# Layer 0 attention: the two heads' score and maximum products interleaved, and the first averages moved

## What is computed

```python
def _gn(v, G=32, eps=1e-5):
    B_, H_, W_, C_ = v.shape
    g = v.reshape(B_, H_, W_, G, C_ // G)
    m = jnp.mean(g, axis=(1, 2, 4), keepdims=True)
    s = jnp.var(g, axis=(1, 2, 4), keepdims=True)
    return ((g - m) / jnp.sqrt(s + eps)).reshape(v.shape)

# layer 0, after q, k, v = heads(x @ W + b)
attn = jnp.einsum('bqd,bkd->bqk', q, k) / np.sqrt(HD)
attn = (attn.reshape(b * NH, h, w, h, w) + rel_bias_h[:, :, :, :, None] + rel_bias_w[:, :, :, None, :])
attn = jax.nn.softmax(attn.reshape(b * NH, hw, hw), axis=-1)
out = jnp.einsum('bqk,bkd->bqd', attn, v)

x = x + _L0_conv_ref(_gn(x), ...)
x = x + _L1_conv_ref(_gn(x), ...)
```

## Time and profile before

| | us |
|---|---|
| median of 3 runs | 3215.44 (3212.84 to 3217.96) |
| the profiled execution, its own time | 3214.5 |
| its span | 3212.7 |

### The profile page before, as it was taken

The page is one execution under the profiler, slowest core; times in us unless marked ns, Lnnn a source line. Parts: engine busy times, 40 slices in busy tenths (PEclk is TensorE's granted clock), DMA queues, the critical chain, the costliest instruction groups (busy, mean ns, idle before and its releaser), DMA issues.

```text
span 3212.7 us, 48955 instructions
## 1 busy us (share of the span) xinstructions
PE 3144.4 (98%) x20428; PEld 2349.5 (73%) x20428; DVE 1703.3 (53%) x1889; ACT 1225.6 (38%) x1397; POOL 1084.7 (34%) x618
## 2 busy tenths in 40 slices
PE   8999999999999999999999999999999999999999
PEld 6875658887787656888778766688777866668876
DVE  4447745446435774543734577444463457744434
ACT  2345542124234654213423465321342355532132
POOL 0037770025003786002400477600330057750042
PEclk9999999999999999999999999999999999999999
DMA  3211013114421101311432100221153111031113
GB/s 124 93 35 26 20 49 115 40 54 130 139 95 27 25 20 50 114 40 61 159 126 72 34 21 18 84 90 40 59 174 108 66 37 24 14 111 59 40 34 115
DMA packets 170520, 220.39 MB, mean 69 GB/s; under 512 B 113856, under 2 KB 126400, under 8 KB 170304
## 3 DMA queue, kind: packets, MB, share of 16 engines
q1 hardware_dynamic: 168768, 215.68, 21.4%
q10 hardware_dynamic: 1536, 1.57, 0.2%
HBM read 141.70 MB, written 50.33 MB: 60 GB/s over the span
## 4 chain that ended last, share of the span: by engine, by line
PE 89%; issue 4%; ACT 3%; POOL 2%; DVE 1%; DMA 0%; SPq 0%; ACTq 0%; POOLq 0%
PE score L1157 15%; PE score L1158 14%; PE score L1159 14%; PE lot L1314 13%; PE score L1279 10%; PE lot L1229 5%; PE lot L1232 3%; PE score L1286 3%; PE score L1292 2%; PE lot L1331 2%; POOL acc L568 2%; PE lot L1262 2%; ACT prob L748 1%; PE lot L1200 1%; PE lot L1157 1%
## 5 line engine op out<-in xcount | busy, mean ns | idle before, releaser
L568 POOL TENSOR_TENSOR acc<-acc,prob 128x1024 f32<-128x1024 f32 x288 | 712.9, 2475 | 208.1 <-ACT prob L748 180.9
L748 ACT ACTIVATE prob<-score 128x1024 f32<-128x1024 f32 (+3 forms) x576 | 517.6, 910 | 416.6 <-PE score L1292 292.6
L889 DVE TENSOR_REDUCE max_part<-lot 128x1 f32<-128x512 f32 x640 | 411.3, 685 | 156.3 <-PE lot L1232 156.3
L1157 PE MATMUL score<-a_hi,w_hi 128*128 128x512 f32 x1152 | 458.9, 398 | 12.9 <-DVE q_lo L1002 5.1
L1314 PE MATMUL lot<-prob,v 128*64 128x512 f32 (+4 forms) x2496 | 462.2, 513 | 5.3 <-ACT o_raw L647 3.7
L1158 PE MATMUL score<-a_lo,w_hi 128*128 128x512 f32 x1152 | 450.7, 391 | 0.0
L1159 PE MATMUL score<-a_hi,w_lo 128*128 128x512 f32 x1152 | 450.0, 391 | 0.0
L568 POOL TENSOR_TENSOR acc<-prob 128x1024 f32<-128x1024 f32 x48 | 120.1, 2502 | 833.6 <-ACT prob L748 833.6
L1157 PE MATMUL score<-w_hi,a_hi 128*128 128x256 f32 x1152 | 336.1, 292 | 0.0
L1314 PEld LDWEIGHTS lot<-prob,v 128*64 128x64 f32 x2496 | 165.6, 137 | 232.0 <-issue 193.0
L1158 PE MATMUL score<-w_lo,a_hi 128*128 128x256 f32 x1152 | 325.5, 283 | 0.0
(11 more groups left out here) (112 smaller groups left out, 5370.2 us busy)
## 6 DMA issues: line engine op xcount, KB each, us to landing
raw<-weights SPq DMA_DIRECT2D x96, 768.0 KB, 4.4
g_mem<-g SPq DMA_DIRECT2D x24, 1024.0 KB, 4.7
xin<-x_t SPq DMA_DIRECT2D x24, 512.0 KB, 6.4
xr<-x_t SPq DMA_DIRECT2D x24, 512.0 KB, 5.2
x_mem<-xr SPq DMA_DIRECT2D x24, 512.0 KB, 6.6
xr<-x_mem SPq DMA_DIRECT2D x24, 512.0 KB, 5.4
y_t<-xr SPq DMA_DIRECT2D x24, 512.0 KB, 6.9
recip<-recip SPq DMA_DIRECT2D x368, 32.0 KB, 1.9
```

Of the source, the lines that this page charges most:

```text
L568: nc.gpsimd.tensor_tensor(acc[:, :, a:b], with_, now, ALU.add).then_inc(added, 1)
L748: nc.scalar.activation(prob[:, ug % P_SLOTS, :, 0:b - a], score[:, u % 2, :, 0:b - a], ACT.Exp, scale=SCALE).then_inc(prob_ok, 1)
L889: nc.vector.reduce_max(max_part[:, t, part, h:h + 1], lot[:, (2 * n + h) % 3, :], AX.X)\
L1157: nc.tensor.matmul(out, w[0], a[0], start=first, stop=False)
```

## The change

It has three parts. (1) At a unit with a maximum ahead, the maximum and the scores are issued as seven mixed pairs: first the two products of head 0's maximum beside head 1's first two score products, then the scores of head 0 beside those of head 1 and, last, head 0's last two score products beside head 1's maximum. Each head of a maximum has its own wait for a bank (two halves back, `no - 2`) and its own signal (`half_mm`), for which DVE waits head by head. (2) At the start TensorE makes six products of ones into `score`, whose result nothing reads. (3) DVE takes the first group's differences right behind its aggregates and its variance behind the fourth tile's statistics, and TensorE's averages of the second three tiles move behind the second and third input tile of the first product. The reduced numbers of the maxima in the projections of layer 0 and in layer 1 (`max_no`) only rename their count.

```diff
+def max_no(f, p, k):
+    return f // 2 * (2 + PAIRS) * QT + f % 2 * 2 * QT + p * QT + k + 1
...
-                dve.wait_ge(max_mm, unit_no(f, p, k))
                 for h in range(2):
+                    dve.wait_ge(half_mm, 2 * n + h + 1)
                     nc.vector.reduce_max(max_part[:, t, part, h:h + 1], lot[:, (2 * n + h) % 3, :], AX.X)\
...
                 statistics(0, i)
                 if i == 2:
                     aggregate(0, 0)
+                    group_means(0, 0)
                 if i == 3:
-                    group_means(0, 0)
+                    group_variances(0, 0)
+                if i == 4:
+                    norm(0, 0)
+                    norm(0, 1)
+                    input_lo(0, 0)
             aggregate(0, 1)
-            group_variances(0, 0)
-            norm(0, 0)
-            norm(0, 1)
-            input_lo(0, 0)
-            group_means(0, 1)
             norm(0, 2)
             input_lo(0, 1)
             input_lo(0, 2)
+            group_means(0, 1)
             group_variances(0, 1)
...
+            def head_pass(f, n, h, e):
+                p, k = n // (2 * QT) + 1, n % (2 * QT)
+                no = 2 * (n + f // 2 * LAST * 2 * QT) + h
+                if e == 0:
+                    if h == 0:
+                        maximum_ready(f, p, k)
+                    if no > 2:
+                        pe.wait_ge(half_max_ok, no - 2)
+                last = maximum_pass(no % 3, f, p, k, h, e)
+                if e:
+                    last.then_inc(half_mm, 1)
+                    halves_issued[0] = no + 1
...
+                banks_free(int(u in (2, 10)))
+                pe.wait_ge(max_ok, maxima_issued[0])
+                for k in range(passes + 2):
+                    if k < 2:
+                        head_pass(f, n, 0, k)
+                    else:
+                        last = score_pass(k - 2, 0)
+                    if k == passes + 1:
+                        last.then_inc(score_ok, 1)
+                    if k < passes:
+                        bias_ready(k)
+                        score_pass(k, 1)
+                    else:
+                        head_pass(f, n, 1, k - passes)
...
+            pe.wait_ge(const_ok, 1)
+            one_column = ones[:, 0:1]
+            for n in range(WARM_UP):
+                nc.tensor.matmul(score[:, 0, 0, :], one_column.to_broadcast([128, 128]),
+                                 one_column.to_broadcast([128, HALF]), start=True, stop=True)
             mean_averages(0, 0)
             shift_averages(0, 0)
-            mean_averages(0, 1)
...
-                        if f % 2 and j == 0 and i == 1:
+                        if len(norm_parts(f)) > 1 and j == 0 and i == 1:
                             mean_averages(f, 1)
-                        if len(norm_parts(f)) > 1 and j == 0 and i == (2 if f else 0):
+                        if len(norm_parts(f)) > 1 and j == 0 and i == 2:
                             shift_averages(f, 1)
...
-                        for n in before:
-                            head_maximum(f, n, int(u in (2, 10)))
-                        scores(f, p, u)
+                        scores(f, p, u, *before)
                         for n in behind:
-                            head_maximum(f, n, 0)
+                            head_maximum(f, n)
```

More of the change, by code:

```diff
@@ L36 @@
 GROUPED = 4
+WARM_UP = 6
 ORDER = (list(range(QT)), [0, 7, 1, 6, 2, 5, 3, 4])
@@ L1217, in maxima_read, with maximum_ready, maximum_pass @@
                     pe.wait_ge(half_max_ok, halves_issued[0])
[L1219 to L1222 removed]
+            def maximum_ready(f, p, k):
                 if k == 0:
                     pe.wait_ge(b_first, first_no(f, p))
[L1225 removed]
+                    if f % 2:
                         pe.wait_ge(qk_hi_ok, f * TILES + CT + p + 1)
[L1227 to L1234 removed]
+            def maximum_pass(bank, f, p, k, h, e):
+                t, _, a, b = max_at(f % 2, k)
+                queries, rows = slice(t * 128, (t + 1) * 128), rows_of(h)
+                bias = b_lo[0] if f % 2 else b_hi[SET_OF[0][p]]
+                w, x = (bias[rows, queries], onehot[rows, a:b]) if e else (
+                    q_hi[rows, p, queries], k_hi[rows, p, a:b])
+                return nc.tensor.matmul(lot[:, bank, 0:b - a], w, x, start=(e == 0), stop=(e == 1))
             def maximum(f, p, k):
@@ L1272, in scores, with score_pass, bias_ready @@
                 ug = units_before(f, p) + u
+                passes = 4 if layer else 5
+                def score_pass(k, h):
+                    w = (k_hi, k_hi, k_lo, None, None)[k]
+                    x = (q_hi, q_lo, q_hi, b_hi[s], b_lo[s])[k]
+                    if k < 3:
+                        w, x = w[rows_of(h), p, keys], x[rows_of(h), p, a:b]
+                    else:
+                        w, x = onehot[rows_of(h), keys], x[rows_of(h), a:b]
+                    return nc.tensor.matmul(score[:, slot, h, 0:b - a], w, x,
+                                            start=(k == 0), stop=(k == passes - 1))
+                def bias_ready(k):
+                    if u == 0 and k == 3:
+                        pe.wait_ge(shifted, pair_no(f, p))
+                        if layer == 0:
+                            pe.wait_ge(b_hi_ok, f // 2 * PAIRS + p + 1)
+                    if u == 0 and k == 4:
+                        pe.wait_ge(b_lo_ok, f // 2 * PAIRS + p + 1)
                 if p == 0 and u < 2:
```

63 lines of the change are left out of this document (21 added, 42 removed).

## The result

| | us |
|---|---|
| before, median of 10 runs | 3213.93 (3209.02 to 3217.96) |
| the change, median of 10 runs | 3205.69 (3203.17 to 3208.82) |
| ratio | 0.9972, 95% interval 0.9964 to 0.9980 |
| the change, profiled execution | 3206.56, span 3204.8 |

The change is faster by 8.2 us, 0.28%. The forecast was 3217 us with a range from 3207, and no change: both were wrong. The first rival's second half names this time (3205) and both causes, but its number is partly luck: start and attention gained some 13 us, more than its 9, and falls of the clock, which it did not have, gave 5 back. One execution of `maximum_moved` (6,176 us) and two of the kernel before (4,639 and 7,379 us) took far longer than all others, and the ratios leave them out.

What follows compares the result with a forecast made beforehand. TensorE, busy 98% of the span, was taken as the bound. Start +2.6 us and attention 0 on the profiled 3214.5 us made 3217 us, no change that can be told, with a range of 3207 to 3224.

Steps and rivals of the forecast that it cites:

- The first rival's second half: Attention waits fall, maxima behind cost nothing, and the clock rises during the first twelve products: 3205 us; whole rival 0.15, half faster.
- The start: Time up to the dense products: first product 3.6 us sooner, given back by averages, late `a_lo` and slow products; +2.6 us.
- if the clock again takes 5.3 us, 12 run at 0.43: Start, behind the last averages: of 54 products left, 12 run at half clock and 42 at 0.227 us, to 48.9 us.
- the late second `a_lo`: Start, after the first six products: DVE delivers the second `a_lo` at 23.3 us, leaving TensorE 1.0 us idle.
- The chain to the first product: Start: line 843 runs ahead of POOL, the power starts at 15.55 us, and the first product at about 19.8, not 23.40.
- The lower bound (-4.6): Start's gain if the clock never falls after the ones: -4.6 us.
- The attention: Layer 0's attention: removed waits and the cost of maxima behind cancel; 0.0 us per image, between -1.8 and +1.3.
- The wait for v and unit 2 together: Attention's first pair: unit 0's scores wait for v, +0.3 us; unit 2's wait for a maximum's read shrinks, -0.5 us.
- Unit 15: Attention: TensorE idles while line 923 holds up DVE; waits one half further back save 0.7 us per image.
- Pairs 1 to 4: Attention, unit 4 of each of these pairs: a later bank removes 0.22 us each, -0.9 us for four.
- So +0.13 in 14 of the 15 cases, +1.8: Attention, maxima behind at u = 1, 5, 9: second head waits for its bank and weight load; +1.8 us per image.
- the fourth rival: Attention: mixed pairs are slower; at 0.005 us a pair it is +9 us, 3226; chance 0.08, three quarters of it slower.

Runs made afterwards that it cites:

- maximum_moved: The change, with the first pair's maximum of unit 14 made behind unit 12 so that DVE's shift is not waited for; 3198.15 us, ratio 0.9943.
- ones_only: The kernel before with only the six products of ones added ahead of the first averages; 3217.68 us, ratio 1.0008.
- mixed_only: The change with its mixed order, but the wait ahead of head 0 of a maximum as long as before; 3235.45 us in one run.
- the ones in the gap: The change with six more float32 products of ones in TensorE's 5.65 us idle time behind the first shift averages; 3207.36 us, ratio 0.9975.
- both averages' places: Two variants of the change: start's second averages behind the first input tile, 3208.93 us; layer 1's end averages behind four output products, 3205.36 us.
- the filled end: The change with one product of ones over 256 columns in the 0.41 us idle time at each end of layer 1; 3205.64 us, ratio 0.9970.
- The last two kernels: The change with unit 14's maximum made behind unit 12, 3198.15 us; the same plus a product of ones at the ends of layer 1, 3197.98 us.
- before_again: The kernel before, unaltered, run and profiled once more; 3213.65 us.
- attention_only: The kernel before with only the change's attention of layer 0, its start as before; 3208.83 us, ratio 0.9984.
- no_ones: The change without the six products of ones at the start; 3211.28 us, ratio 0.9993.

## Why the prediction was wrong

**The start: +2.6 predicted, -4.95 measured.** The failing step is "if the clock again takes 5.3 us, 12 run at 0.43". I had counted from the dense work behind the last averages, because the one rise that I could see stood there; the clock in fact rose over the first twelve products, at 22.6 us, and everything behind ran at full clock. By the step's own terms: the second averages and the shift averages cost 1.48 us each in place of 2.9 and 2.9 (2.8), six products between and six ahead of them 1.5 instead of 2.5 (2.1), the 12 slow products are gone (2.4), the late second `a_lo` costs 0.4 instead of 1.0 (0.6), and the first product is 0.3 early. These make 8.2 us. Against them stands 0.5 us that the forecast had not: at 33.26 TensorE waits for the `a_lo` of the fourth input tile. That leaves 7.7, where forecast and result are 7.55 apart. The chain to the first product was right. The clock was down at the first product, as forecast, but not for the reason given: it fell at 12.4 us, within the shift averages, ahead of the gap. What the forecast said of the ones, that they pay for the first averages alone, was wrong too: `ones_only` has the clock up 8 us earlier than the kernel before and is 3.6 us ahead with nothing else changed. Why ones that end at 8.7 us bring a rise at 26.4, with the clock down between, the runs do not show. The lower bound (-4.6) was near by accident, since it assumed a clock that never fell; in later profiles of the same start the gain is 3.5 to 4.7.

**The attention: 0.0 predicted, -2.0 in each image measured.** The wait for v and unit 2 together: -0.2 predicted, -0.23 measured. Unit 15: -0.7, and -1.04 measured. Pairs 1 to 4: -0.9, and -0.8. These were right. The failing step is "So +0.13 in 14 of the 15 cases, +1.8". The read ends where it was forecast, 1.52 us behind the unit's start (256.20, forecast 1.51). But the maximum behind follows 0.07 us after it, not 0.16 and a weight load, and 0.22 us after the product ahead of it (256.04, 256.26), though the second head's weight load is late: it starts at 256.25, and load and product overlap, as in the earlier trace rows. A unit with its maximum takes 1.58 us (254.68 to 256.26) instead of 1.61, so that mixed pairs, at 0.226 to 0.228 us, are slightly shorter, not longer: the fourth rival was the wrong way round. Over four units with their product with v nothing of this is left, 10.74 us before and with the change (from 285.66 us of the kernel before on); the waits make the whole 2.0. `mixed_only` shows that the effect which I feared exists and costs 0.09 us a time, one half further on.

**What I had not in the sum at all**: the falls of the clock. I had quoted, where the clock fell in the kernel before, and used it only for the start. In the two profiles, four falls for one give back 5 of the 13 us that the change gains. (The sum also left out the 0.9 us by which the median lay above the profiled execution, and which it names; 3218 would have been no nearer.)

**What stays open.** The two profiles of the kernel before have one fall and none, six of the change and its variants with both parts' order kept (the change twice, the ones in the gap, both averages' places, the filled end) have three or four.

But two profiles say too little of the kernel before. Its 74 other executions on record have a mean granted clock of 0.997 to 1.000, 0.9988 on average, and the lower it is, the longer they take: 3211.7 us on average at 1.000 (20 executions), 3217.0 at 0.998 (22). My estimate from this: a mean of 0.9988 is 7.6 us at 1.2 GHz, some two falls in an execution, since one lasts 3.4 us in the windows; the change's ten executions have 0.9964, 23 us, of which the start has 10.2, so some three and a half. By this the falls cost the change some 2.5 us more than the kernel before, not 5, and part of the way from 13 to 8 us stays unexplained.

All 49 falls behind the start in the profiles stand at one of four kinds of place: the end of layer 1 (0.40 us of idle time, then averages of 4 columns), the shift of a first pair (1.36 us idle), the last pair of layer 1's attention (1.26 us idle for ACT's `prob`, then 0.2), and averages of 2 columns with 0.3 to 2.0 us idle. Most such places pass without a fall. The last two kernels, with the second kind taken away, have one fall each in their profiles. That a filled place has none, and that the falls move from it, rests on one profile each. Why the kernel before, with the same light places, falls less often stays open. With the change the falls at the ends of images are 795.3 us apart, so that each image meets the clock as the last did; but the images of the kernel before follow after 795.1 and 794.8 us too, so that this decides it is a guess.

## What to carry to other kernels

A stage that runs at half clock is not only priced by its length: ask what work stands together while the clock is low, and keep narrow averages and idle time out of the first wide products. A wait that hides another must be priced again when the order changes: the mixed order takes 5.8 us more in an image with the old wait than with the new one. And when a gain of 13 us shows as 8, look through the granted clock along the whole span, not only where the diff is, and at the mean clock of all runs, not of two profiles; a stall that stands in the list of waits with 5.4 us in 4 waits was worth 7.5 us, nearly as much as the whole change.

## What the runs showed of the hardware

- The granted clock of a window is 1.00 in the profile of a kernel until the first change of the clock is recorded: in `before_again`, the window from 29.40 to 32.80 (below) has 1.00 while its products are 0.43 us apart, and in the change, whose clock rose with the ones and fell, 19.20 to 22.60 has 0.50 with the same products. The distance of two products tells the level, the column does not.

```profile
29.40:32.80 3.40, 3.40 (x9) 2.63 (x9) 2.58 (x3) 2.01 (x2) 0.38 (x1) 1.00 0.02 5
```

- The clock fell at 766 us behind 0.41 us of idle time and 1.7 us of averages, with no long gap. The Trainium skill ("TensorE: Matmul & The Clock Gate", "A second HAM failure mode: psum-queue depth-cycling") tells of a kernel in which short idle times between groups of matmuls made the clock go up and down; the place at 766 us agrees with that, and the kernel before, with the same 0.41 us and no fall, shows that it does not do so each time.
- A DVE operation on 128x3 elements took 2.92 us at 12.71 beside a POOL operation on two tensors, and 0.16 us ahead of it: it took 2.3 to 2.9 us, to the end of POOL's, wherever it started behind it, in four profiles (before, `attention_only`, `no_ones`, `ones_only`).
- Six products of ones that end at 8.7 us, nothing else changed, moved the rise of the clock from 34.3 to 26.4 us (before, `ones_only`), with 0.50 of the clock between 13.6 and 23.8.
